# Expert runs of 256 rows: gate and up products in one PSUM bank per chunk, and the GpSimd split of the down weights put behind the run

## The reference

```
xn  = layernorm(x)
out = x + attention(xn) + experts(xn)

experts(xn):  logits = xn @ gate_w.T;  the 2 best of 8 experts for each row (of logits + beta)
              c = sigmoid(logits) of these two
              h = silu(xn @ gate_proj_w[e]) * (xn @ up_proj_w[e])     256 -> 512 values
              routed = sum over the two of c * (h @ down_proj_w[e])   512 -> 256 values
              shared = the same with one shared expert, for every row
```

## Time and profile before

| | |
|---|---|
| median of three runs | 1782.52 us |
| profiled execution, own time | 1778.87 us |
| its span | 1777.1 us |
| mean granted TensorE clock | 0.959 |
| TensorE busy, matmuls | 1591.4 us (90%) |
| VectorE busy | 1142.8 us (64%) |
| ScalarE busy | 988.3 us (56%) |
| GpSimd busy | 1112.2 us (63%) |

### The profile page before, as it was taken

One profiled execution on the slowest core, in us unless ns is written; L12 is line 12 of the kernel. 1 busy time (PEld: TensorE's weight loads), 2 busy tenths in 40 slices (PEclk: granted clock), 3 DMA queues, 4 the chain that ended last, 5 costly groups with the idle time before them and its releaser, 6 DMA issues.

```text
span 1777.1 us, 39164 instructions
## 1 busy us (share of the span) xinstructions
PE 1591.4 (90%) x11446; PEld 1288.0 (72%) x11446; DVE 1142.8 (64%) x3885; ACT 988.3 (56%) x2050; POOL 1112.2 (63%) x1165
## 2 busy tenths in 40 slices
PE   5888885999999999999997899989999989999987
PEld 4666665888888888888886566666666666666666
DVE  5999974666666666666665656666566666666652
ACT  4666644454445544455443466666665666666664
POOL 0777775334444333434331478888988988888888
PEclk9999987999999999999998689999999999999999
DMA  4677657444545454454454467776665766667742
GB/s 144 221 245 244 231 228 247 156 155 155 163 153 162 151 163 155 154 162 154 151 154 122 97 137 157 168 166 158 155 164 146 160 147 144 153 155 157 164 122 82
DMA packets 228609, 288.91 MB, mean 163 GB/s; under 512 B 59513, under 2 KB 146170, under 8 KB 228538
## 3 DMA queue, kind: packets, MB, share of 16 engines
q1 hardware_dynamic: 170090, 207.30, 42.2%
q10 hardware_dynamic: 45488, 45.36, 8.5%
q0 software_dynamic: 12960, 35.41, 7.7%
HBM read 198.07 MB, written 79.95 MB: 156 GB/s over the span
## 4 chain that ended last, share of the span: by engine, by line
PE 48%; DVE 16%; POOL 14%; issue 12%; ACT 6%; ACTq 3%; DMA 1%; DVEq 0%; POOLq 0%
PE psum L157 26%; PE psum L950 9%; PE psum L1506 4%; PE psum L1466 4%; POOL plain_arena L1390 3%; POOL plain_arena L1415 3%; POOL plain_arena L1388 3%; ACT plain_arena L1620 2%; DVE split_arena L1193 2%; PE psum L1489 2%; DVE split_arena L734 2%; POOL plain_arena L1428 1%; DVE stats L635 1%; PE psum L1082 1%; DVE plain_arena L1198 1%
## 5 line engine op out<-in xcount | busy, mean ns | idle before, releaser
L157 PE MATMUL psum<-split_arena 128*128 128x512 f32 (+2 forms) x4752 | 971.1, 354 | 19.3 <-DVE split_arena L1175 7.4
L157 PEld LDWEIGHTS psum<-split_arena 128*128 128x128 f32 x4752 | 762.1, 195 | 153.0 <-issue 26.5
L1729 DVE CUSTOM_DVE_ANT_0 plain_arena<-psum,mask 128x256 f32<-128x256 f32 (+1 forms) x1024 | 339.0, 386 | 244.8 <-PE psum L1466 233.7
L1620 ACT ACTIVATE plain_arena<-psum 128x512 f32<-128x512 f32 (+1 forms) x512 | 250.0, 540 | 232.1 <-PE psum L1489 207.2
L1052 POOL TENSOR_TENSOR split_arena<-plain_arena,split_arena 128x1024 fp32r<-128x1024 f32 x43 | 102.8, 2390 | 336.7 <-ACT split_arena L1114 336.7
L1139 ACT ACTIVATE plain_arena<-psum 128x512 f32<-128x512 f32 (+1 forms) x172 | 90.2, 525 | 272.2 <-PE psum L157 251.8
L950 PE MATMUL psum<-split_arena 128*128 128x256 f32 x1704 | 220.1, 286 | 12.7 <-DVE split_arena L1193 12.7
L950 PEld LDWEIGHTS psum<-split_arena 128*128 128x128 f32 x1704 | 208.3, 191 | 16.8 <-DVE split_arena L1193 15.5
L1198 DVE TENSOR_TENSOR plain_arena<-psum,plain_arena 128x512 f32<-128x512 f32 (+1 forms) x172 | 102.7, 597 | 153.0 <-ACT plain_arena L1139 135.8
L1044 POOL DMA_INDIRECT plain_arena<-xn_d,run_ix x142 | 137.2, 967 | 69.2 <-POOL run_ix L1041 35.2
L1466 PE MATMUL psum<-split_arena 48*128 48x256 f32 (+1 forms) x1024 | 155.2, 348 | 13.7 <-POOL plain_arena L1452 7.6
(11 more groups left out here) (202 smaller groups left out, 1936.6 us busy)
## 6 DMA issues: line engine op xcount, KB each, us to landing
plain_arena<-in_gate_w SPq DMA_DIRECT2D x43, 512.0 KB, 3.4
plain_arena<-in_up_w SPq DMA_DIRECT2D x43, 512.0 KB
plain_arena<-in_down_w SPq DMA_DIRECT2D x43, 512.0 KB
plain_arena<-in_x SPq DMA_DIRECT2D x32, 512.0 KB, 7.6
q_d<-split_arena SPq DMA_DIRECT2D x32, 512.0 KB, 3.3
k_d<-split_arena SPq DMA_DIRECT2D x32, 512.0 KB, 4.6
split_arena<-q_d SPq DMA_DIRECT2D x128, 128.0 KB, 3.8
split_arena<-k_d SPq DMA_DIRECT2D x128, 128.0 KB, 4.0
```

Source lines behind the costliest of these rows:

```text
L157: last = pe.matmul(out, lhs_t(p), rhs(q), start=(begins and c == 0 and k == 0), stop=(ends and c == len(chunks) - 1 and k == 2), skip_grou ...
L1620: act.activation(b_pt[:, g % 2, 2 * p + par, 4 * half:4 * half + n, :].rearrange("p k s -> p (k s)"), psum[:, 2 + par, 0:n * P], ACT.Exp, ...
L1729: last = dve.tensor_tensor_reduce(b_junk[:, 2 * par + i % 2, 0:cols], psum[:, par, at:at + cols], mask[:, 2 * P - cols:2 * P], -1.0, 3e38, ...
```

## The change

For narrow runs only, three things change.

1. Gate and up products of chunk m go to the two halves of one bank, bank m, so the four chunks of a narrow run take the banks 0 to 3. TensorE then waits only ahead of chunks 0 and 2, and only for VectorE's products of the run before.
2. ScalarE writes the high part of the next run's down weights after the high part of the next run's rows, no longer behind chunk 2.
3. GpSimd gathers the rows of run n + 2 first, then waits until the down product of run n is done (`c_dn`), and only then writes the low part of the down weights of run n + 1.

```diff
-        def gate_up(pe, m, banks, cols, w, xt):
+        def gate_up(pe, m, out, w, xt):
             for n in range(2):
-                last = split_products(pe, psum[:, banks[n], 0:cols], [
+                last = split_products(pe, out(m, n), [
...
+        def product(m, n, wide):
+            if wide:
+                return psum[:, 2 * (m % 2) + n, :]
+            return psum[:, m, n * HALF:(n + 1) * HALF]
...
 (c_gpsimd)
-                n, _, _, _ = run(i, k)
-                down_lo(i, k + 1)
+                n, wide, _, _ = run(i, k)
+                if wide:
+                    down_lo(i, k + 1)
                 if not (isinstance(n, int) and n == NRUN - 2):
                     pool.wait_ge(c_tr, n + 2)
                     gather(i + (k + 2) // len(RUNS), (k + 2) % len(RUNS))
+                if not wide:
+                    pool.wait_ge(c_dn, n + 2)
+                    down_lo(i, k + 1)
...
 (c_tensor)
                 for m in range(MC):
-                    pe.wait_ge(c_mul, 4 * n + m + 1)
-                    gate_up(pe, m, (2 * (m % 2), 2 * (m % 2) + 1), cols, w,
+                    if wide:
+                        pe.wait_ge(c_mul, 4 * n + m + 1)
+                    elif m % 2 == 0:
+                        pe.wait_ge(c_mul, 4 * n + m // 2 + 1)
+                    gate_up(pe, m, lambda m, n: product(m, n, wide), w,
...
 (c_scalar)
-                    act.activation(c_sg[:, m % 2, 0:cols], psum[:, 2 * (m % 2), 0:cols], ACT.Silu).then_inc(c_silu, 1)
+                    act.activation(c_sg[:, m % 2, 0:cols], product(m, 0, wide), ACT.Silu).then_inc(c_silu, 1)
...
-                    if more and m < 3:
+                    if more and m < (3 if wide else 2):
                         w_hi(1 - u, m, n + 1)
                 hid_hi(MC - 1)
                 if more:
                     x_hi(1 - u, n + 1, run(i, k + 1)[1])
+                    if not wide:
+                        w_hi(1 - u, 2, n + 1)
...
 (c_vector)
-                    dve.tensor_tensor(c_hf[:, m % 2, 0:cols], psum[:, 2 * (m % 2) + 1, 0:cols],
+                    dve.tensor_tensor(c_hf[:, m % 2, 0:cols], product(m, 1, wide),
```

## The result

| | before | changed |
|---|---|---|
| median without a profile | 1782.38 us (1777.42 to 1782.74, 4 runs) | 1758.68 us (1755.03 to 1762.87, 4 runs) |
| profiled execution, own time | 1778.87 us | 1755.03 us |
| span | 1777.1 us | 1753.3 us |

The ratio is 0.9857 (95% interval 0.9836 to 0.9877): 23.7 us faster in the medians (21.9 to 29.2 by the interval), 23.8 us in the profiled executions. The prediction said 1753.7 us in 1747 to 1762.

What follows compares the result with a forecast made beforehand. VectorE's chain, stalled 2.05 us by GpSimd's split, was taken to end each narrow run in a TensorE-bound stage; 14 x 2.06 = 28.8 us off 1778.87 gave 1750.1, as median 1753.7 us, range 1747 to 1762.

Steps and rivals of the forecast that it cites:

- What bounds: Expert stage: TensorE busy 631 of 656 us, but VectorE's chain ends each narrow run, which loses 2.7 us of TensorE time.
- (a): Narrow runs, `down_lo` moved out: `hid_lo` of chunk 1 takes 0.42 instead of 2.47 us, everything behind it 2.06 us earlier.
- (b): Narrow runs, one bank per chunk: waits of 0.22 and 0.38 us go; nothing alone, 0 to 0.3 us a run otherwise.
- (c): GpSimd, gathers before `down_lo`, which then meets `w_lo` in the wide run; `w_lo` waits 0.7 us, cover 0.9, cost 0.
- (d): SyncE's down load, issued later behind `down_lo`: ScalarE may wait up to 0.8 us, 2.0 us of cover, cost 0.
- signs that I had named: Wrong if `down_lo` precedes down product's end, wide runs behind narrow exceed 17.7 us, or ScalarE waits over 2 us for in_down_w.
- the late load: Wide runs, slower rival: down weights land 10 us after issue, TensorE loses 3.8 us a run; 1807 us in all; 4%.
- The sum: Expert stage: 14 x 2.06 = 28.8 us off 1778.87 gives 1750.1 profiled, 1753.7 us as median without a profile.
- The closing run: Closing narrow run of the expert stage: no gap worth the name, gives 0.
- back to back: Rival in narrow runs: TensorE without waits, `x_lo` ending 0.6 us earlier than in the forecast chain; 1745.1 us; 5%.
- The stall did land on `w_lo`: Rival in wide runs: slower gathers put `down_lo` just ahead of `w_lo`, chunk 3 waits 0.7 us; 1764 us; 9%.
- That it is GpSimd: Opposed by a rival: `hid_lo` of chunk 1 keeps its 2.47 us, only the banks' gain is left; 1780 us; 4%.

Runs made afterwards that it cites:

- the order alone: Kernel before with only ScalarE's and GpSimd's new order, banks and TensorE's waits as before; 1753.28 us, ratio 0.9870 to the kernel before.
- the split beside `x_lo`: Changed kernel, but ScalarE's high split back behind chunk 2 and GpSimd's split ahead of the gathers, behind the last `hid_lo`; 1748.89 us, ratio 0.9848.
- the second: The changed kernel measured again without any edit, against the kernel before on the same chip; 1747.25 against 1774.88 us, ratio 0.9843.
- the run with the banks only: Kernel before with only one bank for each chunk in narrow runs and TensorE's changed waits; 1781.88 us, ratio 1.0039 to the kernel before.
- the down load held back: Changed kernel, SyncE's down load in 14 wide runs behind narrow ones waiting for VectorE's product of chunk 2; 1797.27 us, ratio 1.0120.
- the one with the filler: Kernel before with the new banks and 12 extra discarded matmuls in each of 14 narrow runs' down products; 1776.47 us, ratio 1.0001.

## Why the prediction was right, point by point

**What bounds.** Right: VectorE's chain sets a narrow run's end, and the time is won in the 14 narrow runs alone.

**(a) The split out of the narrow run.** Right in mechanism and size. With the banks, all 14 runs gain 2.04 to 2.06 us, so the sum is no luck. From the start of the narrow run, forecast and measured: product of chunk 3 at 7.51 and 7.52 us, end of `x_lo` at 10.18 and 10.19, next gate product at 10.41 and 10.42. Shown by the order alone and by the split beside `x_lo`.

**(b) The banks.** With (a) 0.22 us a run, inside the 0 to 0.3. Wrong for the part by itself: I wrote that it would give nothing alone; it costs 7 us. I had counted what TensorE waits for and not how its waits lie together, and had taken the clock of 1.00 as given.

**(c) GpSimd's order.** The split was to start 13.3 us after the narrow run does and `w_lo` to end at 17.0: 13.4 and 17.0 in the run shown. `w_lo` was to take up to 1.9 us; the longest took 2.34, and the cover held. The new wait never decides. What the step missed is a gather 4 us late once in the stage, a row that the trace of before had (the longest wait of the indirect DMA for "issue" is 4.1 us), and that I did not put behind the new order.

**(d) SyncE.** The issue was forecast at 15.7, measured at 15.9. The cover was mis-sized: 1.0 us instead of 2.0, and so one late gather costs 2.1 us. I had measured it to the last `hid_lo` and the last quarter of the down product. TensorE stops halfway, for the `hid_lo` before it, and the two take 0.74 us longer, because the late high split puts GpSimd's split beside them. Two of the signs that I had named for a wrong forecast (a wide run behind a narrow one over 17.7 us, ScalarE waiting more than 2 us for the down weights) came up in this one run of the 14, not in the others. As a rival the late load decides from 1 us earlier than I had it; that it can make the kernel slower than before is shown (+1.2%).

**The sum.** 28.8 forecast, 28.77 in the trace. The measured 23.7 in the first comparison, 27.6 in the second, and 26.8 without the wait for the down product are this less the late gather, and what the first stage and the first run happened to take. That the last two vary with the execution is seen; why, is open. The closing run, put at nothing, gave 0.2. The last wait of TensorE is 0.40 us and not the 0.6 forecast; the down product ahead of it takes 3.46 us instead of 3.13.

**The rivals.** TensorE is not back to back: it still waits for `x_lo`. The stall did land on `w_lo`, and cost nothing, even where `w_lo` took 2.8 us (order only). That it is GpSimd is shown by the split beside `x_lo`. The late load came once, behind a gather that the forecast had not priced.

## What to carry to other kernels

A wait is worth removing only on the chain that ends last, and on an engine behind that chain it can do harm: it draws short pauses together into one, and TensorE may come out of it at a lower clock. Where GpSimd splits or adds SBUF tiles, place it beside VectorE instructions that read one input from PSUM, and look at which work stands behind it in its queue and in the queues that wait for it. Before work is put behind a row of DMA issues, look at the longest of them, not at the mean.

## What the runs showed of the hardware

- In the run with the banks only, TensorE stood for 1.7 to 2.2 us in each of 14 narrow runs of an otherwise full stretch. The granted clock fell just behind nine of these pauses and a little later behind a tenth. In the order-only run it fell behind one pause of 2.90 us. With the down load held back it fell in or behind eight of 14 pauses of 2.3 to 4.1 us. It stayed at 1.00 behind the other pauses of these runs, behind the one pause of 1.70 to 1.95 us in each of five other traces, and where the pauses were 0.9 us and less (the kernel before, and the one with the filler). What decides it for a pause of about 2 us is open.
- One of the expert stage's 142 indirect DMA issues starts 3.6 to 4.5 us after the one before it has ended, where 0.30 is usual. In all eleven traces it is the same one, the 114th, whatever is placed around it. Why that one is open; it wasn't tried with fewer gathers.
